# Cross-attention kernel on one core: TensorE does the context product ahead of the half output group in an attention step

## The reference, cut to what matters

```python
Q = (hidden_states @ Wq.T + bq).reshape(B, L, NH, HD)
K = (vision_features @ Wk.T + bk).reshape(B, Vn, NH, HD)
Vv = (vision_features @ Wv.T + bv).reshape(B, Vn, NH, HD)
scores = jnp.einsum('blhd,bvhd->bhlv', Q, K) / np.sqrt(HD)
scores = jnp.where(mask, scores, -jnp.inf)
attn = jax.nn.softmax(scores, axis=-1)
ctx = jnp.einsum('bhlv,bvhd->blhd', attn, Vv).reshape(B, L, H)
x = hidden_states + ctx @ Wo.T + bo
# then layer norm of x with ln_g and ln_b
```

## Time and profile before

| | |
|---|---|
| time, median of 3 runs | 739.31 us |
| time of the profiled execution | 738.63 us |
| its span in the trace | 736.8 us |
| TensorE matmuls busy | 698.5 us (95%) |
| VectorE busy | 507.0 us (69%) |
| ScalarE busy | 323.3 us (44%) |
| GpSimd busy | 307.8 us (42%) |
| mean granted clock of TensorE | 0.985 |

### The profile page before, as it was taken

The page is one execution under the profiler, slowest core; times in us unless marked ns, Lnnn a source line. Parts: engine busy times, 40 slices in busy tenths (PEclk is TensorE's granted clock), DMA queues, the critical chain, the costliest instruction groups (busy, mean ns, idle before and its releaser), DMA issues.

```text
span 736.8 us, 14456 instructions
## 1 busy us (share of the span) xinstructions
PE 698.5 (95%) x4764; PEld 638.7 (87%) x4764; DVE 507.0 (69%) x1170; ACT 323.3 (44%) x1061; POOL 307.8 (42%) x343
## 2 busy tenths in 40 slices
PE   9999999999999999999988879999998999999993
PEld 7885699999999999999978768888887888888882
DVE  2547347364745647374667898999999988998733
ACT  0412221212121222112126897777776868777511
POOL 1011022221212212221234685478667876787644
PEclk9999999999999999999999989999999999999997
DMA  8984212513130312211141462013312242222311
GB/s 280 391 294 159 85 58 75 199 44 130 44 114 28 114 57 80 77 43 71 43 115 58 141 188 88 34 51 117 102 44 87 86 117 85 86 85 72 115 58 57
DMA packets 57012, 76.83 MB, mean 104 GB/s; under 512 B 17025, under 2 KB 38657, under 8 KB 56961
## 3 DMA queue, kind: packets, MB, share of 16 engines
q1 hardware_dynamic: 56960, 76.21, 31.0%
HBM read 48.94 MB, written 27.26 MB: 103 GB/s over the span
## 4 chain that ended last, share of the span: by engine, by line
PE 72%; DVE 15%; issue 5%; ACT 5%; DMA 2%; POOL 0%; DVEq 0%; SPq 0%; ACTq 0%
PE ps L503 19%; PE ps L505 19%; PE ps L504 19%; PE ps L606 4%; PE ps L514 3%; PE ps L593 2%; DVE kbd_lo L820 2%; DVE s_sb L842 2%; PE ps L635 2%; PE ps L533 2%; DVE p_lo L859 2%; DVE vbd_lo L829 1%; ACT s_sb L1029 1%; PE ps L568 1%; DMA keys<-k_sb 1%
## 5 line engine op out<-in xcount | busy, mean ns | idle before, releaser
L503 PE MATMUL ps<-act_hi,w_hi 128*128 128x256 f32 x512 | 149.6, 292 | 0.6 <-issue 0.6
L505 PE MATMUL ps<-act_hi,w_lo 128*128 128x256 f32 x512 | 146.2, 286 | 0.0
L504 PE MATMUL ps<-act_lo,w_hi 128*128 128x256 f32 x512 | 146.1, 285 | 0.0
L1106 POOL TENSOR_TENSOR h_t<-pos,neg 128x256 f32<-128x256 f32 x64 | 48.3, 754 | 233.1 <-DVE neg L751 233.1
L503 PE MATMUL ps<-w_hi,act_hi 128*128 128x512 f32 x256 | 105.3, 411 | 4.1 <-DVE act_lo L864 4.1
L955 ACT ACTIVATE act_hi<-h_t 128x256 fp32r<-128x256 f32 x64 | 26.7, 417 | 174.7 <-DVE h_t L758 174.7
L505 PE MATMUL ps<-w_hi,act_lo 128*128 128x512 f32 x256 | 100.4, 392 | 0.0
L504 PE MATMUL ps<-w_lo,act_hi 128*128 128x512 f32 x256 | 100.2, 391 | 0.0
L503 PEld LDWEIGHTS ps<-act_hi,w_hi 128*128 128x128 f32 x512 | 99.4, 194 | 0.8 <-issue 0.8
L1029 ACT ACTIVATE s_sb<-s_sb,s_min 128x64 f32<-128x64 f32 x256 | 85.8, 339 | 31.8 <-DVE s_min L847 31.2
L504 PEld LDWEIGHTS ps<-act_lo,w_hi 128*128 128x128 f32 x512 | 99.4, 194 | 0.0
(11 more groups left out here) (105 smaller groups left out, 1731.1 us busy)
## 6 DMA issues: line engine op xcount, KB each, us to landing
x_sb<-xT SPq DMA_DIRECT2D x8, 1024.0 KB, 6.0
h_rows<-hn_sb SPq DMA_DIRECT2D x32, 256.0 KB, 2.2
q_cols<-q_sb SPq DMA_DIRECT2D x32, 256.0 KB, 2.1
q_raw<-q_cols SPq DMA_DIRECT2D x32, 256.0 KB, 3.2
z_sb<-h_rows SPq DMA_DIRECT2D x16, 512.0 KB, 3.5
out<-z_sb SPq DMA_DIRECT2D x16, 512.0 KB, 2.9
wk_raw<-WkT SPq DMA_DIRECT2D x8, 512.0 KB, 8.4
wv_raw<-WvT SPq DMA_DIRECT2D x2, 2048.0 KB, 11.4
```

The costliest lines, as they stand in the source:

```text
L503: pe.matmul(dst, lh, rh, start=(first and j == 0), stop=False)
L504: pe.matmul(dst, lh, rl, start=False, stop=False)
L505: mm = pe.matmul(dst, ll, rh, start=False, stop=(last and j == n - 1))
L1106: pool.tensor_tensor(h_t[m % 4][:], pos[m % 2][:], neg[m % 2][:], ALU.add).then_inc(sign_ready, 1)
```

## The change

In TensorE's `step`, the call of `context(i, m - 6)` is put ahead of the half output group. Before, the order was scores, transposes, half output group, context product; after, it is scores, transposes, context product, half output group. No instruction is added or taken away, and no wait is changed. The other engines' lists are the same.

```diff
@@ -662,14 +662,14 @@
                     scores(i, m - 2)
                 if live(i, m - 5, CB):
                     p_transposed(i, m - 5)
+                if live(i, m - 6, CB):
+                    context(i, m - 6)
                 group, part = output_group(m)
                 if live(i, group, 8):
                     if isinstance(i, int) and 8 * i + group < 2 and part == 0:

                         pe.wait_ge(stage_lo, RC + KC + 4 * (8 * i + group + 1))
                     projection(i, group, part)
-                if live(i, m - 6, CB):
-                    context(i, m - 6)
```

## The result

The changed kernel takes 741.99 us (median of 9 runs, 740.72 to 742.93) against 738.3 us for the kernel before (median of 9 runs, 736.33 to 739.56). The ratio is 1.0052, with a 95% interval of 1.0037 to 1.0067, so the change costs 3.8 us by the ratio, 2.7 to 4.9 by the interval. 744.2 was forecast as 4.9 us over a median of 739.3. The size of the step is 1.1 us less than forecast. 741.99 lies in the stated range (740.3 to 748.3) but under the narrower band that was called the forecast (742.7 to 746), partly because the kernel before came out 1.0 us lower over nine runs than over three.

What follows compares the result with a forecast made beforehand. TensorE was taken to set the pace in light steps, VectorE in heavy ones. Step 14 of batch 0 and batches 1 to 3 gave 0.48 + 1.28 + 1.28 + 1.86 = 4.9 us; 739.3 + 4.9 = 744.2, range 740.3 to 748.3.

Steps and rivals of the forecast that it cites:

- step 7: Half group's wait for `act_lo` falls away: 0.98 us off the lateness of 2.84 in batch 3, 1.90 in batches 1 and 2.
- light steps: Steps without VectorE's low halves: the earlier context product costs nothing, `p_lo` being over a microsecond early.
- Step by step, batch 3: TensorE's lateness: +0.56 in step 2, +1.57 in step 4, +0.71 in step 5, -0.98 in step 7; 1.86 us remain.
- The restart, 0.11 for each stall,: A context product that waited takes 0.82 us instead of 0.71, so each stall costs 0.11 more.
- Batches 1 and 2: Heavy steps: 2.84 late, less 1.90 for the removed wait, plus 0.34 in step 7; 1.28 us each.
- a stall of 0.23 and its restart come back: Step 7 of batches 1 and 2: `p_lo` at 485.2 against a product due at 485.00; adds 0.34 us.
- Step 14 of batch 0: First step with a half group: product due 439.39, `p_lo` ends 439.71; stall 0.37 plus restart 0.11, 0.48 us.
- Change of neighbours, costed at nothing,: Every changed step: a 512-column matmul stands beside 256-column ones in both orders, so the change of neighbours costs 0.
- The clock: Forecast had no clock term; rival: half clock in each heavy stretch, 1.8 us three times, 5.4, giving 749.6; chance 0.05.
- hidden after all: Rival: heavy stretches are VectorE's length, so stalls fall into time lost anyway; within 0.2%, about 739 to 741; chance 0.11.
- faster: Rival: waits for `act_lo` (4.1 us) and `p_lo` (1.0) vanish with nothing in their place; about 735; chance 0.08.
- Held back longer: Rival: late scores hold VectorE over 0.57 us, step 7's wait returns whole; 9.0 us, 746 to 749; chance 0.14.

Runs made afterwards that it cites:

- The experiments by step: New order in some steps only, against the kernel before: steps 11 to 15, 0 and 1 ratio 1.0001; 2 to 7 ratio 1.0051; 8 to 10 ratio 1.0031.
- the pair without low halves: VectorE makes no low halves of keys and values, waits go to the high halves; against the kernel before: old order 722.86 us, new order 723.38 us.
- the kernel with the product in the middle: Context product between two quarters of the output group in all steps, against the kernel before: 737.54 against 736.81 us, ratio 1.0006.
- the kernel with the light steps moved: New order only in steps 11 to 15, 0 and 1, against the kernel before: 736.8 against 736.81 us, ratio 1.0001.
- the thinned kernel in the new order: New order, VectorE's low halves of keys and values made for one chunk of four, against the kernel before: 730.01 against 737.13 us.
- the first four experiments: New order in steps 11 to 1, 2 to 7 or 8 to 10 only, and product mid-group, against the kernel before: 736.8, 740.58, 739.18, 737.54 us.

## Why the prediction was right, point by point

**The mechanism** held: the context product waits for `p_lo` in steps 2, 4 and 5 of batches 1 to 3, the old wait of step 7 falls away and that of step 5 is taken over by the larger one, VectorE waits for scores in step 6 (0.38 to 0.39 us in all three batches), and the lateness is not won back. One statement on the way was wrong and did no harm: light steps were said to cost nothing because `p_lo` is over a microsecond early. In steps 8 to 10 of the old order it is up to 0.6 late for the new place, which cost 2.3 us when these steps alone were changed; in the changed kernel TensorE's own lateness covers it. The experiments by step show the place (steps 2 to 7 cost all of it, 11 to 1 nothing), the pair without low halves shows the cause (VectorE's lateness, not the order itself), and the kernel with the product in the middle shows that only the part of the lateness counts that exceeds the wait of step 7.

**Step by step, batch 3.** Shifts of the first transpose from one step to the next, forecast and measured: step 2 0.56 and 0.47; step 4 1.57 and 1.58; step 5 0.71 and 0.72; step 7 -0.98 and -0.91. In sum 1.86 forecast, 1.83 measured (from 2.55 late in step 2 to 4.38 in step 8).

**The restart, 0.11 for each stall,** was mis-sized. A product that waited takes 0.82, but in the new order one that doesn't wait takes 0.80 too, since the transposes stand before it; 0.71 holds only behind a half group. So a restart costs 0.02 here. A smaller restart makes the next stall longer by the same amount, as the end of `p_lo` stays where it is, so only the last restart counts: TensorE is 2.73, 2.74 and 2.74 late before step 7 of batches 1, 2 and 3, not 2.84.

**Step 7 came out right in batch 3 with some luck.** What sizes its wait is a thing that the prediction didn't look at: how long the half of step 6, just ahead of `ctx_low` and `p_low` on VectorE, takes. Kernel before, batches 2 and 3, with GpSimd's next instruction:

```profile
558.28 2.00 DVE L829 TENSOR_TENSOR vbd_lo<-v_b,vbd_hi 64x128 fp32r<-64x128 f32 x4
558.77 0.74 POOL L1119 TENSOR_TENSOR q_lo<-q_raw,q_hi 128x256 fp32r<-128x256 f32 x1 [0.27 <-ACT q_hi L1021]
...
636.25 1.08 DVE L829 TENSOR_TENSOR vbd_lo<-v_b,vbd_hi 64x128 fp32r<-64x128 f32 x4
637.17 0.76 POOL L1119 TENSOR_TENSOR q_lo<-q_raw,q_hi 128x256 fp32r<-128x256 f32 x1 [0.71 <-ACT q_hi L1021]
```

The 0.92 between 2.00 and 1.08 is the 0.92 between the waits of 1.90 and 0.98. It isn't a property of a batch: in the kernel with the light steps moved the half took 1.08 in batch 2 and 1.61 in batch 3, and the wait was 0.99 and 1.51. So what a batch has to take off its lateness changes from one execution to the next. Changed kernel, batch 3:

```profile
639.29 1.85 DVE L829 TENSOR_TENSOR vbd_lo<-v_b,vbd_hi 64x128 fp32r<-64x128 f32 x4
...
642.10 0.68 DVE L859 TENSOR_TENSOR p_lo<-ps,p_hi 128x512 fp32r<-128x512 f32 x1
```

The half took 0.77 longer than in the kernel before, and `p_lo` came 1.26 late instead of the forecast 0.57. That used up the margin of 0.75 that the prediction had there, and the product at 642.83 waited 0.09 for it.

**Batches 1 and 2: the term mis-sized.** Forecast were 1.28 each; measured, from the first transpose of step 2 to that of step 8, 0.90 and 0.93. About 0.1 of that is the last restart. The rest is "a stall of 0.23 and its restart come back" in step 7: there the product starts 0.45 to 0.46 after the first transpose in batches 1 and 2, a stall of 0.10 and no restart that could be told. VectorE was held back by 0.47 and not 0.57, and its half of step 6 took 1.85 and not 2.00 us, so `p_lo` came 0.32 to 0.34 late.

**Step 14 of batch 0** was to cost 0.48 and cost nothing: steps 13 and 14 together take 10.31 us after (4.99 and 5.32) and 10.30 before (4.68 and 5.62). What step 14 seems to win, step 13 loses; half clock sets in 0.3 us earlier in the changed kernel's trace. The step that failed is "due 439.39": I had added 0.36 us, the pace at full clock, to a row that stands in a window with a clock of 0.50. The row behind it in the trace of before says 0.71, so the product would have been due at 439.74, and `p_lo` ended at 439.71:

```profile
439.74 0.78 PE L503 MATMUL ps<-w_hi,act_hi 128*128 128x512 f32 x1
```

Changed kernel, same place:

```profile
440.16 1.06 PE L635 MATMUL ps<-ident,s_sb 128*128 128x128 f32 x4
440.86 0.56 PE L503 MATMUL ps<-p_hi,vbd_hi 128*128 128x256 f32 x1
```

At half clock the transposes take 0.70 and `p_lo` (ended 440.55) is ready. In the thinned kernel in the new order this step ran at full clock (1.00 from 436 to 440 us), and there a stall is seen: 438.16 for the product, 436.87 for the transpose, 0.93 more than 0.36. So the term comes and goes with the clock.

**Change of neighbours, costed at nothing,** is nearly that: the product gets 0.09 longer behind the transposes and the half group 0.09 shorter behind the product (2.75 for 2.84), and a step as a whole 0.01 shorter, which is 0.2 us a batch by the pair without low halves.

**The sum.** From step 15 of batch 0 to the end of the steps the changed kernel's trace is 3.5 us longer, and before that the two are equal from the first softmax transpose on. The 1.4 us between 4.9 and 3.5 are 0.48 for step 14, 0.38 and 0.35 for batches 1 and 2, 0.03 for batch 3, and 0.1 for the light steps. The 3.8 us of the runs has an interval of 2.7 to 4.9, so its distance from 3.5 says nothing.

**The clock** stayed at 1.00 in the heavy stretches of all three batches of the changed kernel. Its window 569 to 647 us, with the earlier trace rows beside it:

```profile
569.00:647.00 78.00, 74.28 (x444) 65.20 (x442) 70.77 (x151) 57.37 (x217) 57.57 (x64) 1.00 0.28 88
```

TensorE's busy time is the same to half a microsecond in a batch that is longer. The drop at the start of the half groups is in both traces. The rivals: hidden after all and faster are ruled out by the interval, which begins at 1.0037, and the clock by this row. Held back longer is ruled out as far as its size of 9.0 us goes; VectorE was held back longer than forecast in batch 3, but by its own half of step 6 and not by late scores.

What stays open is why the kernel before has medians from 736.8 to 738.3 in the different comparisons (the first four experiments ran on one chip and the other eight on another), how much of that is the length of the half of step 6, and why spreading the values' halves lengthens batch 0; none of it was tried further. No version that keeps all the work beat the kernel before: the light steps alone in the new order are equal to the kernel before.

## What to carry to other kernels

Where two engines each set the pace for a part of a period, the instruction that waits for the other engine is best put late in the step: work without a wait, put ahead of it, is the cover. Of the three places tried here the end of the step was the cheapest and the middle cost 0.4 us, which is within the noise. To cost such a move, take the slack of each step at the new place, carry the lateness from step to step, and take off the waits that the lateness swallows; an average over the steps, or the slack of a single step by itself, gives neither the place nor the size. Take the pace of a step from rows at the same clock, and the size of a wait that is to be swallowed from more than one period or execution: here it was 0.98, 1.51 or 1.90 us.

## What the runs showed of the hardware that I had not expected

VectorE's subtraction `kbd_lo` of two SBUF operands took 0.41 us when it started beside an idle GpSimd and 1.17 and 1.41 beside a GpSimd that was at work without a pause; the same four instructions took 2.49 and 3.94 us. The four of `vbd_lo` in step 6 took 1.08, 1.61 or 2.00 us in the old order with no change to them, by where GpSimd's instructions fell, and the stop of TensorE in step 7 was each time 0.1 us shorter than that (0.98, 1.51, 1.90). Placing the half of step 3 some 1.9 us later within its step, and two other halves behind `p_low` as well, without changing one of them, made the kernel 6.3 us slower; the longer instructions are seen in the trace, and their share of the 6.3 was not measured by itself.
